# Causal attention on TensorE: the weighting of the values taken for two query tiles at once, in four of the eight steps of a unit

## What is computed

```python
xn = (x - mu) / sqrt(var + 1e-05) * ln_gamma + ln_beta
q, k, v = split(einsum('bnd,ed->bne', xn, w_qkv), 3)      # 16 heads of 64
sim = einsum('bhid,bhjd->bhij', q * scale, k)
sim = where(causal, mask_value, sim)                      # j > i is masked
attn = softmax(sim - max(sim))
out = einsum('bhij,bhjd->bhid', attn, v)
x = einsum('bne,de->bnd', out, w_out) + b_out             # (the kernel adds x)
```

## Time and profile before

| | |
|---|---|
| median of 3 runs | 4156.67 us (4153.51 to 4160.11) |
| the profiled execution | 4156.45 us, span 4154.6 us |
| mean granted TensorE clock | 0.962 |
| busy share of the span | PE 86%, PE weight loads 56%, DVE 56%, ACT 63%, POOL 21% |
| value products (L1468) | 4608 instructions on PE |

### The profile page before, as it was taken

How to read it: one execution, slowest core, us unless ns; L and a number is a source line. 1 busy time by engine, 2 the same in 40 slices (tenths; PEclk the granted TensorE clock), 3 DMA queues, 4 the chain that set the end, 5 groups by cost and what they waited for, 6 DMA issues and landing times. The chain is left out here.

```text
span 4154.6 us, 78799 instructions
## 1 busy us (share of the span) xinstructions
PE 3573.7 (86%) x28532; PEld 2337.7 (56%) x28596; DVE 2310.2 (56%) x4748; ACT 2622.2 (63%) x5190; POOL 866.4 (21%) x850
## 2 busy tenths in 40 slices
PE   6699998688887888859999999999977888788886
PEld 4222225466664666636666666666655666556664
DVE  4100003676666766665555555555566667676676
ACT  2599994476766676745555555555536667666665
POOL 1000000221112112123333333333322212122111
PEclk9899999899998999979999999999989999999999
DMA  1122220100000000000000000000000000000000
GB/s 30 28 39 39 36 36 6 34 0 0 0 0 28 0 0 0 0 11 7 7 8 5 8 8 5 8 6 7 8 7 29 0 0 0 20 8 0 0 0 20
DMA packets 35833, 46.27 MB, mean 11 GB/s; under 512 B 7840, under 2 KB 28192, under 8 KB 35232
## 3 DMA queue, kind: packets, MB, share of 16 engines
q1 hardware_dynamic: 34304, 40.23, 4.7%
q10 hardware_dynamic: 1440, 4.85, 0.3%
HBM read 25.13 MB, written 2.10 MB: 7 GB/s over the span
## 5 line engine op out<-in xcount | busy, mean ns | idle before, releaser
L793 POOL TENSOR_TENSOR rot<-cosine,sine 128x1024 f32<-128x1024 f32 x144 | 339.4, 2357 | 1615.3 <-DVE sine L1102 1615.3
L1608 ACT ACTIVATE e<-e,nmax 128x768 f32<-128x768 f32 (+7 forms) x512 | 396.0, 774 | 434.6 <-DVE e L1534 431.5
L1643 POOL TENSOR_SCALAR e<-e,inv 128x768 f32<-128x768 f32 (+7 forms) x512 | 375.2, 745 | 845.1 <-DVE inv L1539 845.1
L530 ACT ACTIVATE e<-slot 128x1024 f32<-128x1024 f32 x512 | 472.5, 1087 | 39.2 <-PE slot L466 39.2
L1534 DVE TENSOR_SCALAR_CACHE_REDUCE e<-slot 128x768 f32<-128x768 f32 (+7 forms) x512 | 375.6, 752 | 162.1 <-PE slot L1444 162.1
L1455 PE MATMUL slot<-ident,e 128*128 128x128 f32 x2304 | 354.8, 281 | 32.5 <-DVE eT L1527 28.3
L1438 PE MATMUL slot<-key,q 64*128 64x512 f32 (+3 forms) x1536 | 317.2, 518 | 38.2 <-DVE e L1534 37.0
L834 PE MATMUL slot<-w_qk,hT 128*128 128x512 f32 x576 | 303.8, 656 | 26.6 <-DMA w_qk<-in_local_w_qk_dram 19.0
L1527 DVE COPY eT<-slot 128x512 f32<-128x512 f32 (+3 forms) x384 | 237.7, 619 | 149.5 <-PE slot L1455 149.5
L1455 PEld LDWEIGHTS slot<-ident,e 128*128 128x128 f32 x2304 | 251.7, 141 | 113.1 <-issue 47.8
L1468 PE MATMUL slot<-eT,v 128*64 128x128 f32 x4608 | 307.9, 278 | 0.0
(11 more groups left out here) (178 smaller groups left out, 7067.5 us busy)
## 6 DMA issues: line engine op xcount, KB each, us to landing
w_qkv<-in_causal_w_dram SPq DMA_DIRECT2D x32, 192.0 KB
query<-q_hi SPq DMA_DIRECT2D x128, 32.0 KB
keys<-q_hi SPq DMA_DIRECT2D x128, 32.0 KB
query<-q_lo SPq DMA_DIRECT2D x128, 32.0 KB
keys<-q_lo SPq DMA_DIRECT2D x128, 32.0 KB
tables<-in_const_angles_dram ACTq DMA_DIRECT2D x4, 1024.0 KB, 5.7
X<-in_x_dram SPq DMA_DIRECT2D x4, 512.0 KB, 7.2
w_qk<-in_local_w_qk_dram SPq DMA_DIRECT2D x4, 512.0 KB
```

What stands on the lines that cost most here:

```text
L530: act.activation(e[n % E_RING][:], c.slots[n % RING][:].rearrange(flat), ACT.Exp, scale=2 * SCALE).then_inc(e_ready, 1)
L793: pool.tensor_tensor(rot[:, j, :, :].rearrange(flat), cosine[j % 2][:], sine[j % 2][:], ALU.add)\
L1608: act.activation(part, part, ACT.Exp, bias=nmax[:, n, h:h + 1], scale=-1.0, accum_out=total[:, n, h:h + 1]).then_inc(e_ready, 1)
L1643: pool.tensor_scalar(part, part, inv[:, n, h:h + 1], 1.0, ALU.mult, ALU.mult).then_inc(scaled, 1)
```

## The change

The values are weighted in four steps instead of eight. `values(n)` is called for n = 2, 3, 6 and 7 alone, and each call does two query tiles: that of step n and that of step n - 2. For the key tiles that both need, one product has 256 columns (both query tiles); for the one key tile that only the longer needs, one product has 128. The pairs are tiles (7, 6), (0, 1), (5, 4) and (2, 3). For this the eight `eT` buffers become two tensors with the set as a dimension, so that the columns of two sets can be read by one instruction with a stride, and the tiles of `o` are placed in another order (`place`), so that both tiles of a pair lie side by side.

```diff
+    def place(n):
+        return 4 * (1 - n % 2) + n // 2
...
-        eT = [[sb(f"eT{r}{h}", [P, S]) for h in range(2)] for r in range(RING)]
+        eT = [sb(f"eT{h}", [P, RING, TPB, P]) for h in range(2)]
...
                 def values(u, k, n, first):
-                    i = tile_of(n)
-                    if n in (0, 1) and not first:
-                        pe.wait_ge(x_ready, 2 * u - (n == 0))
+                    pair = (n - 2, n)
+                    shared = min(tile_of(m) for m in pair) + 1
+                    if n in (2, 3) and not first:
+                        pe.wait_ge(x_ready, 2 * u - (n == 2))
                     for bank in range(2):
                         pe.wait_ge(eT_out[bank], chunks(u, n, 1 if wide(n) else bank, bank) + 1)
-                    for t in range(i + 1):
+                    slot = n % RING % 2
+                    for t in range(shared):
                         for h in range(2):
-                            m = pe.matmul(o[64 * h:64 * h + 64, i // 4, (i % 4) * P:(i % 4 + 1) * P],
-                                          v[k][:, t, 64 * h:64 * h + 64], eT[n % RING][h][:, t * P:(t + 1) * P],
-                                          start=(t == 0), stop=(t == i), skip_group_check=True)
-                    if i in (4, 3):
+                            m = pe.matmul(o[64 * h:64 * h + 64, place(n - 2) // 4, place(n - 2) % 4 * P:(place(n - 2) % 4 + 2) * P],
+                                          v[k][:, t, 64 * h:64 * h + 64], eT[h][:, slot:slot + 3:2, t, :],
+                                          start=(t == 0), stop=False, skip_group_check=True)
+                    longer = max(pair, key=tile_of)
+                    for h in range(2):
+                        m = pe.matmul(o[64 * h:64 * h + 64, place(longer) // 4, place(longer) % 4 * P:(place(longer) % 4 + 1) * P],
+                                      v[k][:, shared, 64 * h:64 * h + 64], eT[h][:, longer % RING, shared, :],
+                                      start=False, stop=True, skip_group_check=True)
+                    if n in (6, 7):
                         m.then_inc(o_ready, 1)
...
                     if n - V_LAG >= 0 or not first:
                         uv, kv, nv = earlier(u, k, n - V_LAG)
-                        values(uv, kv, nv, first and n - V_LAG >= 0)
+                        if nv in (2, 3, 6, 7):
+                            values(uv, kv, nv, first and n - V_LAG >= 0)
```

More of the change, by code:

```diff
@@ L1479, in output @@
                     for t in range(4):
-                        m = pe.matmul(o[:, bank, t * P:(t + 1) * P], oT[:, (4 * bank + t) * P:(4 * bank + t + 1) * P],
+                        at = (7 - t if bank else t) * P
+                        m = pe.matmul(o[:, bank, t * P:(t + 1) * P], oT[:, at:at + P],
                                       wo[k][:], start=True, stop=True)
@@ L1516, in _ @@
                         transpose(u, n - T_LAG, 1, False)
-                    values(u, k, n - V_LAG, False)
+                    if n - V_LAG in (6, 7):
+                        values(u, k, n - V_LAG, False)
                 output(u, k, 0)
@@ L1526, in evacuate @@
                             dve.wait_ge(turned[0], chunks(u, n, h, 0) + 1)
-                            dve.tensor_copy(eT[n % RING][h][:, at * P:(at + tiles) * P], turn[:, 0, 0:tiles * P])\
+                            dve.tensor_copy(eT[h][:, n % RING, at:at + tiles, :].rearrange("p t q -> p (t q)"), turn[:, 0, 0:tiles * P])\
                                .then_inc(eT_out[0], 1)
@@ L1601, in evacuate @@
                             act.wait_ge(turned[1], chunks(u, n, h, 1) + 1)
-                            act.activation(eT[n % RING][h][:, at * P:(at + tiles) * P], turn[:, 1, 0:tiles * P],
+                            act.activation(eT[h][:, n % RING, at:at + tiles, :].rearrange("p t q -> p (t q)"), turn[:, 1, 0:tiles * P],
                                            ACT.Copy).then_inc(eT_out[1], 1)
```

## The result

The changed kernel takes 4215.4 us (median of 4, 4212.89 to 4220.73) against 4157.38 us before (median of 4, 4153.51 to 4160.11). The ratio is 1.0142, with a 95% interval of 1.0124 to 1.0160: 1.4% slower, 58 us. The forecast was 4195 (4170 to 4214). The sign was right; the time came out 20 us above the forecast and 1.4 us above the range.

A forecast was written before the change was run, and what follows sets the result against it. PE was taken as the bound except from step 0 to 1 and 4 to 5, where DVE's chain sets the pace. +1.18 us a unit over 30 distances gives 35, plus 3 for the ends: 4156.67 + 38 = 4195 us, range 4170 to 4214.

The forecast's parts named there:

- What bounds the kernel: Causal stage: DVE's chain between scores sets the pace from step 0 to 1 and 4 to 5; PE sets it elsewhere.
- A wide pass costs 0.216, a group without its neighbours' part 0.15: PE's value products: 256-column pass 0.216 us against 0.109 narrow; each group adds 0.15 us fixed, besides transitions of its neighbours.
- The eight intervals: Times between starts of scores of successive steps in a unit: changes sum to +1.18 us, from 39.26 to 40.44.
- the close race: Step 3 to 4: the next scores need ACT's second key copy, ending at 2322.23; PE would be ready at 2322.29.
- The ends, +3: Last unit with what follows it: +3 us; the first distance's changes about cancel.
- Rival 5: The clock falls in PE's longer waits; at 1.5 us lost a unit, 4240 us. Chance 0.02.
- Rival 1: Second half of a wide pass nearly free, kernel faster: 4099 us at 0.109 a pass. Chance 0.03.
- Rivals 2 to 4: 2: own line. 3: no new wait before step 0, 4157 us, chance 0.02. 4: wide passes at 0.235, 4212 us, 0.05.
- Rival 2: PE bounds after all, other engines' chains move up, the whole 1.32 us a unit arrives: 4115 us. Chance 0.03.

The follow-up runs named there:

- one pair undone: Changed kernel with the values of steps 5 and 7 apart and narrow again, the other three pairs kept wide: 4183.61 us, ratio to before 1.0061.
- the filled wait: Changed kernel plus four f32 products that nothing reads at the end of step 0 in each unit but the first: 4206.65 us, ratio to before 1.0111.
- the other wait filled: Changed kernel plus two f32 products that nothing reads at the end of step 7, none added in step 0: 4216.49 us, ratio to before 1.0139.
- the width alone: Changed kernel with its four value groups and buffers, but each 256-column product written as two of 128: 4216.38 us, ratio to before 1.0139.
- one group moved: Kernel before with step 5's values (12 instructions) done in step 1 in place of step 0: 4210.01 us, ratio 1.0122; with the wait filled 4180.73 us, 1.0049.

## Why the prediction was right in sign and wrong in size

- *What bounds the kernel.* Right. DVE's chain sets the intervals 0 to 1 and 4 to 5: they stayed 5.16 and 4.20 in the changed kernel and in every run that put no more work there than fits the waits, whatever was taken out. With more, they grew: 5.43 with six key tiles added in step 0, 5.00 with eight added in step 4.
- *A wide pass costs 0.216, a group without its neighbours' part 0.15.* Right: 2.53 us for the group of step 1, as worked out, and 0.07 us a unit for the whole width. That the 0.15 comes from the change between 128 and 64 weight columns no run isolates.
- *The eight intervals.* The sum was 40.44 and came out at 40.55. The largest misses are 3 to 4 (4.41, measured 4.47; ACT's key copy ends 0.13 us before these scores start, so it is likely the close race that the prediction names) and 7 to 0 (3.46, measured 3.51). The new waits for POOL and ACT are there with 0.51 and 0.37. In the trace 30 x 1.29 = 39 us are what the sum's 35 stood for.
- *The ends, +3.* Mis-sized: 2.2 in the last unit and 4.7 behind it, 2 to 3 of which are the low clock. Its working has a misreading too: "18 key tiles of values left behind its last scores in place of 12". There are 18 in both kernels (before, groups of 24, 12 and 36 instructions of 128 columns). What changes is that the first six no longer stand in front of the waits there, but behind them.
- *Rival 5, the clock.* This is the step that failed. The prediction gave it 0.02, since "in the first unit it waited 2.57 us at once, and behind it the granted clock stayed at 1.00", and concluded "that a wait longer than those to come did not set it off". One wait that passed without a fall was taken as proof for some 30 units, each with two waits in a row, and the sum had nothing for the clock. That it passed was luck: behind the same wait of 2.57 us the clock did fall in the run with one pair undone. The low clock took 13.1 us in the steady part and 2 to 3 at the end. Without them the time would have been near 4200, inside the range. The run with the filled wait, which keeps the low stretch at the end, took 4206.65 beside 4160.98 for the kernel before in its round. The rival was priced at 1.5 us in every unit; a fall cost 1.64, in 8 of 31.
- *The 20 us between forecast and result* are thus 13.1 for the clock in the steady part, 3.3 for the unit (40.55 in place of 40.44, 30 times) and 3.9 for the ends (6.9 in place of 3), of which 2 to 3 are the clock again.
- *Rival 1.* It did not come: in the group of 2.53 us the wide passes start 0.216 us apart, close to twice the 0.109 of a narrow one. The estimate of 0.126 from the Trainium skill's figures ("TensorE: Matmul & The Clock Gate", section "Back-to-back issue gap") is not borne out. The Trainium skill's Part 1 on the same page, that the clock is throttled unless the engine has been busy, fits the runs only in part: the clock fell where PE had been busy for 1.71 of the 3.42 us before, and no longer fell where 0.87 us of work that nothing reads were put in; but in most units it stayed up behind 1.72 of 3.42.
- *Rivals 2 to 4.* None came. Rival 2, PE as the bound all through, is refuted by the runs in both directions: one group fewer made the kernel slower where its work left a wait, and the same work in the same number of groups made it faster where it entered one.

Not settled: why the clock falls in just every fourth unit here, and in 19 of 31 where one group was moved, though the waits in step 0 are alike (1.23 and 1.22). The distances between falls from one step 1 to another are 163.8 us in the changed kernel and with the other wait filled, 163.8 or 204.8 with the width alone, and 41.0 or 81.9 with one group moved. They are all multiples of 41.0 us, which is the length of no unit in these runs (40.55, 40.62 and 39.91, or 41.5 to 42.4 with a fall). Together with the first unit of the run with one pair undone this points to the place of the wait in a rhythm of the clock's own, and not to the wait by itself. No run moved the waits against the clock and left everything else alone, so it is not shown.

## What to carry to other kernels

Work on the busiest engine is not all worth the same: what stands in front of a wait for another engine is free as long as the wait is not used up, and moving it to a place where the engine never waits costs its full time (0.65 us a unit for twelve instructions here), so list the waits of the engine before merging or moving its groups, and count a saving only up to the next one. Turn the finding around as well: here the same list of waits gave a version that is 1.4% faster than before, with the same products. And when a change makes PE's waits longer, price a fall of the clock from what the engine does around them, and do not rule it out by one wait that went well: the same wait went well in ten runs here and not in the eleventh.

## What the runs showed of the hardware

- In 8 of 31 units the granted clock fell to its level of 1.2 GHz for 3.4 us behind two waits of 1.23 and 0.48 us with 0.66 us of transposes between, though PE was 90% busy over the unit (36.62 of 40.55 us). In the other units the same waits brought no fall. f32 products of 512 columns then took 3.21 us for four in place of 1.98.
- The same instructions with the same wait of 2.57 us were followed by a fall in one run and by none in ten others. In that run the clock had risen 4.8 us before the stage's first scores, in the others 3.2 to 3.4.
- Products that nothing reads (0.87 us a unit, in a wait) made a kernel faster, by keeping the clock up: 1.0111 against 1.0142, and 1.0049 against 1.0122 in the pair of runs with one group moved.
- A group of f32 value products (64 weight columns) between transposes (128) costs PE about 0.3 us beside its passes of 0.109 us. Sixteen instructions took 1.02 us from their start to that of the next group and 32 took 1.90, which leaves 0.14 to 0.15 a group; eight transposes behind values took 1.02 and seven behind output products 0.86, which leaves 0.10 for the way out and 0.05 more for the way in. The busy column doesn't show it, since the record of each product (273 ns) is longer than its pitch (109 ns). That the width is the cause is likely, but no run isolates it.
